# One exponential over two PSUM banks in the second pass of a softmax attention stream

## The reference, cut to what matters

```
def adaptive_temperature_softmax(logits):
    original_probs = jax.nn.softmax(logits, axis=-1)
    entropy = jnp.sum(-original_probs * jnp.log(original_probs + 1e-09), axis=-1, keepdims=True)
    ...
    beta = jnp.where(entropy > 0.5, jnp.maximum(poly_result, 1.0), 1.0)
    return jax.nn.softmax(logits * beta, axis=-1)
```

## Time and profile before

| what | value |
|---|---|
| median of 3 runs | 2394.24 us (2392.93 to 2397.34) |
| the profiled execution's own time | 2394.96 us |
| its span | 2393.2 us |
| busy shares of the span | PE 69%, DVE 61%, ACT 58%, POOL 6% |
| instructions of L1355 (the exponential that is changed) | 576, 337.1 us busy, 602 ns mean |

### The profile page before, as it was taken

How to read it: one execution, slowest core, us unless ns; L and a number is a source line. 1 busy time by engine, 2 the same in 40 slices (tenths; PEclk the granted TensorE clock), 3 DMA queues, 4 the chain that set the end, 5 groups by cost and what they waited for, 6 DMA issues and landing times. The chain is left out here.

```text
span 2393.2 us, 22586 instructions
## 1 busy us (share of the span) xinstructions
PE 1649.6 (69%) x6426; PEld 712.0 (30%) x6426; DVE 1468.5 (61%) x3457; ACT 1398.1 (58%) x2634; POOL 143.8 (6%) x127
## 2 busy tenths in 40 slices
PE   4788599999997344778877787777867774122091
PEld 2443244444443001222323222332222222122061
DVE  5554353535344799787797878877787507487211
ACT  4464243434332596989989899798989763000030
POOL 0000000000001000000000000000000000144505
PEclk9898799999998555665567666676666796555596
DMA  3000255555553101101010110201001000200322
GB/s 133 1 0 0 51 151 141 142 144 141 146 149 79 56 24 47 64 19 60 21 72 33 35 54 15 91 20 43 36 31 48 21 28 4 37 0 1 114 62 79
DMA packets 55773, 143.12 MB, mean 60 GB/s; under 512 B 7888, under 2 KB 22608, under 8 KB 53040
## 3 DMA queue, kind: packets, MB, share of 16 engines
q1 hardware_dynamic: 52448, 136.56, 18.9%
q0 software_dynamic: 2048, 4.20, 0.6%
q10 hardware_dynamic: 1152, 0.92, 0.3%
HBM read 124.22 MB, written 17.43 MB: 59 GB/s over the span
## 5 line engine op out<-in xcount | busy, mean ns | idle before, releaser
L1435 DVE CUSTOM_DVE_ANT_0 sa_lg<-sa_e,sa_lg 128x1024 f32<-128x1024 f32 (+7 forms) x512 | 387.1, 756 | 163.7 <-ACT sa_lg L1347 163.5
L1215 PE MATMUL sa_ps<-sa_k1s,sa_q1s 72*128 72x512 bf16 (+3 forms) x768 | 295.8, 454 | 233.6 <-DVE sa_nmax L1426 197.9
L1337 ACT ACTIVATE sa_e<-sa_e,sa_nmax 128x1024 f32<-128x1024 f32 (+7 forms) x512 | 401.2, 784 | 48.5 <-DVE sa_nmax L1426 48.2
L1426 DVE CUSTOM_DVE_ANT_0 sa_e<-sa_ps,sa_mask 128x1024 f32<-128x1024 f32 (+7 forms) x512 | 385.4, 753 | 37.0 <-PE sa_ps L1215 35.3
L1347 ACT ACTIVATE sa_lg<-sa_e,sa_sum 128x1024 f32<-128x1024 f32 (+7 forms) x512 | 400.4, 782 | 2.7 <-DVE sa_prod L1435 2.2
L1355 ACT ACTIVATE sa_p<-sa_ps 128x512 f32<-128x512 f32 x576 | 337.1, 602 | 110.8 <-PE sa_ps L1249 57.5
L1246 PE MATMUL sa_ps<-sa_q2s,sa_k2s 75*128 75x512 bf16 (+3 forms) x768 | 297.4, 424 | 93.6 <-ACT sa_p L1355 71.4
L863 DVE TENSOR_TENSOR mx_hw<-mx_spread,mx_h 128x512 f32<-128x512 f32 x256 | 176.4, 691 | 251.5 <-ACT mx_h L770 242.9
L770 ACT ACTIVATE mx_h<-mx_ps 128x512 f32<-128x512 f32 (+1 forms) x264 | 156.8, 597 | 285.3 <-PE mx_ps L706 277.0
L706 PE MATMUL mx_ps<-mx_f,m 128*128 128x512 f32 x512 | 263.0, 595 | 1.3 <-ACT mx_h L770 1.3
L719 PE MATMUL mx_ps<-mx_hw,m 128*128 128x512 f32 x512 | 262.0, 594 | 1.1 <-DVE mx_hw L863 1.1
(11 more groups left out here) (306 smaller groups left out, 1894.6 us busy)
## 6 DMA issues: line engine op xcount, KB each, us to landing
mx_spread<-mx_spill SPq DMA_DIRECT2D x256, 256.0 KB, 4.0
sa_q1s<-sa_spill_q SPq DMA_DIRECT2D x96, 96.0 KB
sa_k1s<-sa_spill_k SPq DMA_DIRECT2D x96, 96.0 KB
sa_q2s<-sa_spill_q SPq DMA_DIRECT2D x48, 192.0 KB
sa_k2s<-sa_spill_k SPq DMA_DIRECT2D x48, 192.0 KB
m<-m_in SPq DMA_DIRECT2D x1, 4256.0 KB
be_w<-w_in SPq DMA_DIRECT2D x16, 256.0 KB, 6.4
sa_spill_q<-sa_qp SPq DMA_DIRECT2D x4, 768.0 KB, 12.8
```

The lines of the kernel that those rows point to most:

```text
L1215: last = nc.tensor.matmul(out[:, col:col + w], q_ring[:, c % 2, local, i * P:(i + 1) * P], k_ring[:, c % 2, local, col:col + w], start=Tru ...
L1337: nc.scalar.activation(e[:, u % 5, 0:w], e[:, u % 5, 0:w], ACT.Exp, scale=-1.0, bias=nmax[:, b % 2, i, h:h + 1], accum_out=sums[:, b % 2, ...
L1426: nc.vector.tensor_tensor_reduce(out=e[:, u % 5, 0:w], in0=slot_of("unit", u)[:, 0:w], in1=mask_wide[:, SEQ - w:SEQ], scale=1.0, scalar=3. ...
L1435: nc.vector.tensor_tensor_reduce(out=lg[:, u % 2, 0:w], in0=e[:, u % 5, 0:w], in1=lg[:, u % 2, 0:w], scale=1.0, scalar=0.0, op0=ALU.mult, ...
```

## The change

Banks 4 and 5 are now one buffer of 1024 columns. Pieces m (even) and m + 1 fill it, and one ACTIVATE over both banks takes the exponential of the two, for heads hh - 1 and hh of `p_t`. ACT issues it at the place of the odd piece, and does nothing at the place of the even one. PE fills the first half (even m) once the exponential of the pair before has ended, and the second half without a wait of its own. The count of `exp2_ready` is halved to match. The matmuls, the tiles and every other queue stay as they were.

```diff
-                    if m >= 2:
-                        pe.wait_ge(exp2_ready.sem, m - 1)
+                    if m >= 2 and m % 2 == 0:
+                        pe.wait_ge(exp2_ready.sem, m // 2)
                     out, col = ps[:, 4 + m % 2, :], 0
...
-                    pe.wait_ge(exp2_ready.sem, GROUP * (v + 1))
+                    pe.wait_ge(exp2_ready.sem, GROUP // 2 * (v + 1))
...
                     act.wait_ge(s2_mm.sem, m + 1)
                     if v >= 2:
                         act.wait_ge(pv_mm.sem, v - 1)
-                    nc.scalar.activation(p_t[:, v % 2, hh, :], ps[:, 4 + m % 2, :], ACT.Exp, scale=-1.0
+                    nc.scalar.activation(p_t[:, v % 2, hh - 1:hh + 1, :], ps[:, 4:6, :], ACT.Exp, scale=-1.0
                                          ).then_inc(exp2_ready.sem, 1)
...
                     for m in pieces2_at(u):
-                        exp2(m)
+                        if m % 2:
+                            exp2(m)
```

## The result

The changed kernel takes 2416.56 us (median of 5 runs, 2408.58 to 2425.19) against 2393.05 us (5 runs, 2386.76 to 2397.34). The ratio is 1.0097, 95% interval 1.0069 to 1.0125: slower by 1.0%, 23 us, between 16 and 30. Two executions at a much lower clock, one of the kernel with heavier single pieces (2722 us) and one of the kernel before (2586 us), are left out of the ratios further down.

The account below looks back on a forecast made before the run. ACT was taken to set the pace in the middle (91% busy), neither engine to be full in the tail. Middle -7 plus tail +12 gave +5 us, from the median 2399.5, said as 2400; range for 8 in 10, 2385 to 2424.

Parts of the forecast that it names:

- forecast proper: Whole kernel: the prediction's main case, a time of 2399 to 2412 us, chance 0.38.
- second and third rival: Whole kernel: PE becomes the bound in the middle, 2424 us, chance 0.13; PE's clock falls in the tail, 2425, chance 0.07.
- third rival: Tail: PE's longer gaps drop its clock to half, four pieces take 5.15 us, +38 instead of +12, 2425 us; chance 0.07.
- three signs of being wrong: The middle changes by over 12 us either way, the new instruction lasts far from 1.02, or PE's tail clock falls.
- The tail at the full clock: Last two groups, running alone: four pieces take 0.55 us more without mask, 0.65 with one, 0.79 cut; 11.7 us in all.
- the first pieces run at the half clock: Start of the tail: 0.5 us added for PE's half clock, making the tail +12 us.
- The middle: From 950 to 1887 us, where both passes run together: -8 + 5 + 3 - 7 = -7 us.
- the merging, -8: Middle: 241 pairs save 0.053 us of ACT each, 12.8 at most; 60% taken, -8 us, bounds 0 and -12.8.
- The new waits, +5 + 3 - 7 = +1: Middle: PE late in some packs +5; waiting for both pieces at q = 0 and 16 +3; shorter stalls at q = 8 and 24 -7.
- The middle pays for the tail: Middle: full saving of 12.8 us, stalls at q = 8 and 24 gone, PE never late; whole -8, 2386 us; chance 0.18.
- PE becomes the bound in the middle: Middle: the single-buffered chain passes ACT's period in most packs at half clock, +30 instead of +5; whole 2424 us; chance 0.13.
- The cover of the DMA: Before the tail: pieces get 4 us longer but PE's 13.49 us wait for the DMA hides it; cost nothing, otherwise +4.

Follow-up runs that it names:

- heavier single pieces: One more matmul ahead of each piece of the first 14 groups, against the kernel before, single exponentials kept: ratio 1.0060, +14.4 us.
- the pieces at the odd place: Against the kernel with pairs in the first 14 groups only, PE makes both pieces of a pair at the odd one's place: ratio 1.0066 to the kernel before, +15.8 us.
- heavier pieces: One more matmul ahead of each piece of the first 14 groups, against the kernel with pairs there only: ratio 1.0126 to the kernel before; with single exponentials 1.0060.
- second set: The changed kernel run again with nothing changed: ratio 1.0111 to the kernel before, six runs between 2412.7 and 2426.9 us.
- four banks in the tail: Against the kernel before, pieces of the last two groups go round four banks, single exponentials kept: ratio 0.9945, median 2383.06 us.
- filler: Against the changed kernel, two unread matmuls after each tail pair that no answer follows: ratio to the kernel before 1.0084 in both last groups, 1.0079 in the first only.

## Why the prediction was right, and where it was not

The direction and the range held: 2416.6 lies in 2385 to 2424, on the slower side. The size was off: +5 was forecast, +23 (16 to 30) measured. The range held with some luck: 2416.6 lies above the 2399 to 2412 of the forecast proper, in the part that only the second and third rival had put into the range. And of the prediction's own three signs of being wrong one came: PE's clock in the tail fell, from 0.94 to 0.74. Point by point:

- **The tail at the full clock: right.** Forecast 0.55, 0.65 and 0.79 us more for four pieces, 5.85 for a group. Measured at the full clock 0.57 without mask and 0.83 for cut packs, and 31.3 us for the last group against 25.3, +6.0. Two buffers in place of one take it away with the pairs kept, which shows the cause. The loss per pair is what runs one after the other: the second piece, the way from a piece to its exponential, the double exponential, the wait.
- **The clock in the tail: the term that was mis-sized.** The prediction put it at 0.5 us, "the first pieces run at the half clock". If the first group takes that of before plus 6, 38.2 us, wherever the clock comes up as early as before (an estimate), the longer half clock cost 3.2 us in the kernel with pairs in the tail, 4.9 and 13.9 in the two profiled runs of the changed kernel. The third rival had the mechanism and priced it for the whole tail (+26 over the forecast's 12) at a chance of 0.07; its 5.15 us for four pieces at the half clock were measured as 4.96. What came is a part of it, and not the same part in the two profiled runs. Of the 12.3 us between their spans 9.0 lie in this group; 4.9 lie behind the tail, where nothing was changed.
- **The middle: wrong in sign.** Forecast -7, measured +3.4 with pairs in the middle alone, +3.9 in the profile. Of its terms the merging, -8, was worth -1.6 (between +2 and -5 by the intervals). The new waits, +5 + 3 - 7 = +1, cost +5.

The trace shows where a saving goes in a full stretch. Nine pieces to eight units make four pairs and five pairs in turn between two exponentials of 1024 keys. Here are such starts of the changed kernel, with the one stall between them:

```profile
1429.39 1.14 ACT L1337 ACTIVATE sa_e<-sa_e,sa_nmax 128x1024 f32<-128x1024 f32 x1
...
1444.40 1.15 ACT L1337 ACTIVATE sa_e<-sa_e,sa_nmax 128x1024 f32<-128x1024 f32 x1
...
1457.44 1.02 ACT L1355 ACTIVATE sa_p<-sa_ps 128x1024 f32<-128x1024 f32 x1 [0.23 <-PE sa_ps L1246]
...
1460.69 1.14 ACT L1337 ACTIVATE sa_e<-sa_e,sa_nmax 128x1024 f32<-128x1024 f32 x1
```

The three exponentials of L1337 are 15.01 and 16.29 us apart, 31.30 for 16 units. Before, the same two (from 1431.02 to 1462.40) took 15.69 each, 31.38 in all. Without a wait nine pairs would save 9 x 0.053 = 0.48 us; 0.08 are left. The stall in the stretch with five pairs takes 0.23 of the difference; for the other 0.17 the trace shows no wait. The stalls at the units with two pieces, the last two beside those of before:

```profile
1342.78 1.02 ACT L1355 ACTIVATE sa_p<-sa_ps 128x1024 f32<-128x1024 f32 x1 [5.39 <-PE sa_ps L1246]
...
1362.80 1.02 ACT L1355 ACTIVATE sa_p<-sa_ps 128x1024 f32<-128x1024 f32 x1 [0.90 <-PE sa_ps L1249]
1379.02 1.02 ACT L1355 ACTIVATE sa_p<-sa_ps 128x1024 f32<-128x1024 f32 x1 [2.50 <-PE sa_ps L1249]
1394.84 1.02 ACT L1355 ACTIVATE sa_p<-sa_ps 128x1024 f32<-128x1024 f32 x1 [0.69 <-PE sa_ps L1246]
```

```profile
1380.25 1.13 ACT L1355 ACTIVATE sa_p<-sa_ps 128x512 f32<-128x512 f32 x2 [1.23 <-PE sa_ps L1249]
...
1396.37 1.08 ACT L1355 ACTIVATE sa_p<-sa_ps 128x512 f32<-128x512 f32 x2 [0.24 <-PE sa_ps L1246]
```

At 1342.78, behind widen, the wait grew from 4.96 by 0.43, one issue at the half clock, as forecast. At 1362.80 it shrank from 1.75 to 0.90: by half, not to 0.35. At 1379.02, the first pieces of a group, it grew from 1.23 to 2.50, and I had put 0.2 to 0.43 on it. At 1394.84, q = 8, where a shrinking was forecast, it grew from 0.24 to 0.69. The matmul of the first pieces starts when the DMA has landed:

```profile
1379.50 0.61 PE L1246 MATMUL sa_ps<-sa_q2s,sa_k2s 75*128 75x512 bf16 x1 [1.81 <-DMA sa_q2s<-sa_spill_s]
```

```profile
1377.73 0.61 PE L1246 MATMUL sa_ps<-sa_q2s,sa_k2s 75*128 75x512 bf16 x1 [1.43 <-DMA sa_q2s<-sa_spill_s]
```

Of the 1.27 us by which ACT's wait grew, 0.54 is the second piece (from the matmul's start to the exponential 0.75 us before, 1.29 after), and 0.73 is that ACT began to wait 1.21 us before the matmul instead of 0.48. What ACT saves ahead of such a point is not time saved. How the 5 us of the new waits divide between these points, the second piece and the scores that queue behind the waiting piece is open: the pieces at the odd place hardly touched the waits for scores, and the heavier pieces show that the wait for two pieces costs more as a piece gets longer, not what it costs without the extra matmul.

- **The rivals.** "The middle pays for the tail" fell: it gave nothing back. "PE becomes the bound in the middle" is not what happened at +5, but the heavier pieces show how near it is.
- **The price of the instruction: right.** 1.013 us and a distance of 0.06 between the two forms, where 1.02 and 0.053 were forecast. The Trainium skill's page "ScalarE: Activation LUTs" (section "What ACT_TABLE_LOAD costs") has 186 ns beside the columns and 93 ns of overlap between neighbours, from which 0.09 us is an estimate of the saving for each pair; the 0.06 measured decides.
- **The cover of the DMA.** Forecast a wait of about 9.5 us, measured 6.14 (the earlier trace rows has 13.49); the pieces ahead of it ran at the half clock too (0.50 between 1900 and 1910 us, where it was 1.00 before), and got longer by more than the 4 us of my estimate. It still hid them.

What stays open is how much of the 23 us is the clock. The parts measured alone, +3.4 and +12, make 15, by their intervals 10 to 21, and the changed kernel has 16 to 30 (21 to 32 in its second set), so that whether the two parts add up is not settled. How PE comes into the tail does not explain the late clock: with pairs in the middle alone it comes from the same middle with a gap of 6 us, and its clock was up after 5 us. With the ring of two or with four banks in the tail it was up after 4 to 8 us in seven profiles and after 11 in the eighth (heavier pieces, pairs in the middle); with the single buffer and no filler after 12 us in two, 14 and 45. So the late clock goes with the single buffer, by a narrow margin in all but one run. That it is PE's waits that hold it down is argued: the filler, made to show it, narrowed the spread of the runs, but moved the time by no more than the intervals leave open, and there are one or two profiles for each kernel.

## What to carry to other kernels

Merging two instructions saves the fixed part of one (0.05 us here), but if their ring is merged with them, producer and consumer take turns: look for the stage where nothing else stands in their queues, for there the whole turn is the period. Price that stage at both levels of TensorE's clock, since a producer that waits more may also run at the lower one. And a saving on the busiest engine counts only up to the next point at which that engine waits for a DMA or another engine anyway.

## What the runs showed of the hardware

- ACT's exponential over two PSUM banks lasts 1.013 us against 0.603 over one: 0.41 us more, where its further 512 columns come to 0.427 by the slope of the earlier trace rows. Crossing from one bank to the next shows no cost.
- One exponential of 1024 columns takes ACT 0.06 us less than two of 512 from start to start (periods of 1.97 and 2.03 us in the tail).
- PE at 76% to 85% busy stayed at 1.2 GHz for 45 us in one run, and in another of the same kernel, 75% busy, left it after about 14 us. With the filler PE was 93% busy over the first 10 us of the tail at a mean clock of 0.63 in one kernel, and 95% busy at 0.50 in the other; in the kernel with heavier pieces and pairs in the middle it was 98% busy there at 0.50. Two runs of the same kernel differed by 9 us in this one group of 40 to 50 us.
